# The sine product of k: from VectorE on PSUM to GpSimd on a copy in SBUF

## What is computed

```
q, k, v = split(x @ Wqkv)                 # 16 heads of 64
q = l2norm(q) * qs ;  k = l2norm(k) * ksc
q = q*cos*scale   + rotate_half(q)*sin*scale
k = k*cos/scale   + rotate_half(k)*sin/scale
out = softmax(8 * q k^T + mask) v         # window of 32, own and previous
x = out @ Wo + x ;  x = x + feed_forward(shift_tokens(x))
```

## Time and profile before

| | |
|---|---|
| median of 3 runs (lowest, highest) | 3969.29 us (3961.99, 3978.91) |
| the profiled execution | 3966.94 us |
| its span, first to last instruction | 3964.8 us |
| mean granted clock of TensorE, share of full speed | 0.975 |
| TensorE busy | 3450.3 us, 87% |
| VectorE busy | 3145.0 us, 79% |
| ScalarE busy | 2042.6 us, 52% |
| GpSimd busy | 2058.0 us, 52% |
| tiles, rounds of four tiles | 192, 48 |

### The profile page before, as it was taken

One profiled execution on the slowest core, in us unless ns is written; L12 is line 12 of the kernel. 1 busy time (PEld: TensorE's weight loads), 2 busy tenths in 40 slices (PEclk: granted clock), 3 DMA queues, 4 the chain that ended last, 5 costly groups with the idle time before them and its releaser, 6 DMA issues. The chain is left out here.

```text
span 3964.8 us, 101654 instructions
## 1 busy us (share of the span) xinstructions
PE 3450.3 (87%) x42643; PEld 2207.1 (56%) x42643; DVE 3145.0 (79%) x5766; ACT 2042.6 (52%) x3871; POOL 2058.0 (52%) x1073
## 2 busy tenths in 40 slices
PE   8998788888888889888889888888888888888886
PEld 4554455555555555555555555555555555555554
DVE  3334788888788888788888888888888888888885
ACT  2222355555555555555555555555555555555554
POOL 0000565656556555555556556555555565555562
PEclk9999899999999999999999999999999999999999
DMA  2000001000000000001000001000001000000000
GB/s 63 1 1 1 7 10 31 10 7 10 10 15 28 10 10 10 7 15 28 10 10 10 7 15 31 7 10 10 7 15 31 10 7 10 10 15 10 15 10 12
DMA packets 62282, 52.55 MB, mean 13 GB/s; under 512 B 11526, under 2 KB 59396, under 8 KB 61828
## 3 DMA queue, kind: packets, MB, share of 16 engines
q1 hardware_dynamic: 61828, 46.05, 4.3%
HBM read 43.93 MB, written 2.10 MB: 12 GB/s over the span
## 5 line engine op out<-in xcount | busy, mean ns | idle before, releaser
L412 POOL TENSOR_TENSOR cosp<-cosp,sinp 128x1024 f32<-128x1024 f32 x384 | 906.5, 2361 | 801.2 <-DVE sinp L826 801.2
L402 POOL TENSOR_TENSOR cosp<-cosp,rr 128x1024 f32<-128x1024 f32 x384 | 722.9, 1904 | 677.4 <-DVE rr L65 677.4
L694 ACT ACTIVATE sq<-ps 128x1024 f32<-128x1024 f32 x384 | 393.5, 1025 | 1231.1 <-DVE sinp L826 1231.1
L483 PE MATMUL ps<-w_qk,xs 128*128 128x512 f32 x1536 | 769.2, 624 | 51.2 <-ACT xs L683 46.9
L823 DVE TENSOR_TENSOR cosp<-ps,tab 128x1024 f32<-128x1024 f32 x384 | 469.1, 1222 | 386.3 <-PE ps L483 386.3
L588 PEld LDWEIGHTS ps<-px,w_vo 128*128 128x128 f32 x6144 | 715.2, 192 | 94.2 <-issue 89.6
L588 PE MATMUL ps<-px,w_vo 128*128 128x128 f32 x6144 | 717.5, 275 | 0.5
L490 PE MATMUL ps<-ident,cosp 128*128 128x128 f32 x3072 | 438.1, 300 | 308.1 <-DVE hh L846 168.6
L490 PEld LDWEIGHTS ps<-ident,cosp 128*128 128x128 f32 x3072 | 383.2, 155 | 348.5 <-issue 239.0
L483 PEld LDWEIGHTS ps<-w_qk,xs 128*128 128x128 f32 x1536 | 274.5, 199 | 406.0 <-issue 204.8
L826 DVE TENSOR_TENSOR sinp<-ps,tab 128x1024 f32<-128x1024 f32 x384 | 466.3, 1214 | 0.0
(11 more groups left out here) (102 smaller groups left out, 4038.3 us busy)
## 6 DMA issues: line engine op xcount, KB each, us to landing
tab<-in_tab SPq DMA_DIRECT2D x96, 128.0 KB, 2.0
qks<-in_scales SPq DMA_DIRECT2D x96, 128.0 KB, 3.4
w_qk<-in_L_ffn_Wqkv SPq DMA_DIRECT2D x12, 512.0 KB, 6.5
w_v<-in_wv_t SPq DMA_DIRECT2D x6, 512.0 KB, 8.2
w_o<-in_L_ffn_Wo SPq DMA_DIRECT2D x6, 512.0 KB, 9.3
x<-in_L_attn_x SPq DMA_DIRECT2D x16, 128.0 KB, 3.5
out<-w_v SPq DMA_DIRECT2D x16, 128.0 KB, 2.7
w<-in_L_ffn_W SPq DMA_DIRECT2D x6, 341.0 KB
```

Source lines behind the costliest of these rows:

```text
L402: eng.tensor_tensor(v, v, rr[:, B % 2, HEADS * i:HEADS * i + HEADS].unsqueeze(2).to_broadcast([P, HEADS, DH]), ALU.mult).then_inc(rot_read ...
L412: eng.tensor_tensor(cosp[:, A % 2, i, :], cosp[:, A % 2, i, :], sinp[:, i, :], ALU.add).then_inc(rot_added, 1)
L483: t = eng.matmul(ps[:, u, :], xs[:, n % ROUND, :], w_qk[:, n // TILES % 2, i, 512 * u:512 * u + 512], start=True, stop=True)
L694: eng.activation(sq[:, i, :], R.rearrange("p a n -> p (a n)"), ACT.Square).then_inc(sq_done, 1)
```

## The change

The sine product of k leaves VectorE's list. ScalarE copies k from `R` into a new SBUF tensor `kk` after the cosine product of k (`k_cos_done`, and the sine product of the tile before, `k_sin_done`), signals `k_evac`, and squares `kk` in place of `R`. GpSimd makes the sine product from `kk` between its two additions, waits for its own result and for the cosine product, and adds k. The next q projection waits for `k_evac` alone, and the table loads for both products of k.

```diff
@@ sync, load_table
-                    eng.wait_ge(k_roped, 2 * (ROUND * (T - 1) + 2 * w + 2))
+                    eng.wait_ge(k_cos_done, ROUND * (T - 1) + 2 * w + 2)
+                    eng.wait_ge(k_sin_done, ROUND * (T - 1) + 2 * w + 2)
@@ gpsimd, step
-                    for i, roped in enumerate((q_roped, k_roped)):
-                        eng.wait_ge(roped, 2 * A + 2)
-                        eng.tensor_tensor(cosp[:, A % 2, i, :], cosp[:, A % 2, i, :], sinp[:, i, :], ALU.add).then_inc(rot_added, 1)
+                    eng.wait_ge(q_roped, 2 * A + 2)
+                    eng.tensor_tensor(cosp[:, A % 2, 0, :], cosp[:, A % 2, 0, :], sinp[:, 0, :], ALU.add).then_inc(rot_added, 1)
+                    eng.wait_ge(k_evac, A + 1)
+                    after(eng, rot_added, 2 * A)
+                    sin = tab[:, A % ROUND // 2, 3, :].rearrange("p (u f) -> p u f", u=2).unsqueeze(1).to_broadcast([P, HEADS, 2, 32])
+                    eng.tensor_tensor(sinp[:, 1, :].rearrange("p (h u f) -> p h u f", u=2, f=32),
+                                      kk[:, :].rearrange("p (h u f) -> p h u f", u=2, f=32)[:, :, ::-1, :], sin, ALU.mult).then_inc(k_sin_done, 1)
+                    eng.wait_ge(k_cos_done, A + 1)
+                    eng.wait_ge(k_sin_done, A + 1)
+                    eng.tensor_tensor(cosp[:, A % 2, 1, :], cosp[:, A % 2, 1, :], sinp[:, 1, :], ALU.add).then_inc(rot_added, 1)
@@ tensor, step
-                    after(eng, k_roped, 2 * A)
-                    after(eng, sq_done, 2 * A)
+                    after(eng, k_evac, A)
@@ scalar
             def square(n, i):
-                eng.wait_ge((q_roped, k_roped)[i], 2 * n + 2)
                 after(eng, ssq_done, 2 * n - 1 + i)
-                eng.activation(sq[:, i, :], R.rearrange("p a n -> p (a n)"), ACT.Square).then_inc(sq_done, 1)
+                if i == 0:
+                    eng.wait_ge(q_roped, 2 * n + 2)
+                    eng.activation(sq[:, 0, :], R.rearrange("p a n -> p (a n)"), ACT.Square).then_inc(sq_done, 1)
+                else:
+                    eng.wait_ge(k_evac, n + 1)
+                    eng.activation(sq[:, 1, :], kk[:, :], ACT.Square).then_inc(sq_done, 1)
+
+            def take_k(n):
+                eng.wait_ge(k_cos_done, n + 1)
+                after(eng, k_sin_done, n)
+                eng.copy(kk[:, :], R.rearrange("p a n -> p (a n)")).then_inc(k_evac, 1)
...
                 if tile(A):
+                    take_k(A)
                     square(A, 1)
@@ vector, rope
-                eng.tensor_tensor(cosp[:, n % 2, i, :].rearrange("p (h d) -> p h d", d=DH), src, cos, ALU.mult).then_inc(roped, 1)
-                after(eng, rot_added, 2 * n - 1 + i)
-                swapped = R.rearrange("p a (h u f) -> p (a h) u f", u=2, f=32)[:, :, ::-1, :]
-                eng.tensor_tensor(sinp[:, i, :].rearrange("p (h u f) -> p h u f", u=2, f=32), swapped, sin, ALU.mult).then_inc(roped, 1)
+                eng.tensor_tensor(cosp[:, n % 2, i, :].rearrange("p (h d) -> p h d", d=DH), src, cos,
+                                  ALU.mult).then_inc((q_roped, k_cos_done)[i], 1)
+                if i == 0:
+                    sin = tab[:, w, 1, :].rearrange("p (u f) -> p u f", u=2).unsqueeze(1).to_broadcast([P, HEADS, 2, 32])
+                    after(eng, rot_added, 2 * n - 1)
+                    swapped = R.rearrange("p a (h u f) -> p (a h) u f", u=2, f=32)[:, :, ::-1, :]
+                    eng.tensor_tensor(sinp[:, 0, :].rearrange("p (h u f) -> p h u f", u=2, f=32), swapped, sin, ALU.mult).then_inc(q_roped, 1)
```

More of the change, by code:

```diff
@@ L132, in build @@
         sq = sb("sq", [P, 2, INNER])
+        kk = sb("kk", [P, INNER])
         ss = sb("ss", [P, 2 * HEADS + TB])
@@ L215, in build @@
         q_roped = sem("q_roped")
-        k_roped = sem("k_roped")
+        k_cos_done = sem("k_cos_done")
+        k_evac = sem("k_evac")
+        k_sin_done = sem("k_sin_done")
         sq_done = sem("sq_done")
@@ L815, in rope @@
             def rope(n, i):
-                roped = (q_roped, k_roped)[i]
                 w = n % ROUND // 2
@@ L819, in rope @@
                 cos = tab[:, w, 2 * i, :].unsqueeze(1).to_broadcast([P, HEADS, DH])
-                sin = tab[:, w, 2 * i + 1, :].rearrange("p (u f) -> p u f", u=2).unsqueeze(1).to_broadcast([P, HEADS, 2, 32])
                 eng.wait_ge((q_done, k_done)[i], n + 1)
                 after(eng, turned, 4 * (n - 2) + 2 + 2 * i)
-                eng.tensor_tensor(cosp[:, n % 2, i, :].rearrange("p (h d) -> p h d", d=DH), src, cos, ALU.mult).then_inc(roped, 1)
-                after(eng, rot_added, 2 * n - 1 + i)
-                swapped = R.rearrange("p a (h u f) -> p (a h) u f", u=2, f=32)[:, :, ::-1, :]
-                eng.tensor_tensor(sinp[:, i, :].rearrange("p (h u f) -> p h u f", u=2, f=32), swapped, sin, ALU.mult).then_inc(roped, 1)
+                eng.tensor_tensor(cosp[:, n % 2, i, :].rearrange("p (h d) -> p h d", d=DH), src, cos,
[5 more added lines that the diff above has]
+                    eng.tensor_tensor(sinp[:, 0, :].rearrange("p (h u f) -> p h u f", u=2, f=32), swapped, sin, ALU.mult).then_inc(q_roped, 1)
             def square_sum(n, i):
```

## The result

The changed kernel takes 4399.49 us (median of 4 runs, 4398.71 to 4400.33) beside 3965.64 us of the kernel before (4 runs, 3958.53 to 3978.91): 1.109 times as long, 95% interval 1.106 to 1.112. The loss is 434 us; the forecast was 289. The direction and the mechanism came as predicted, the size did not: the time stands at the upper end of the range. The profiled execution took 4400.33 us at a mean granted clock of 0.92, which was 0.975 before.

What follows compares the result with a forecast made beforehand. A loop through VectorE's k products and inverse roots and TensorE's transposes was taken to bound three of four steps; 3967 + 201 (roots waiting for GpSimd) + 88 (clock falls) = 4256 us, range 4100 to 4400.

Steps and rivals of the forecast that it cites:

- rivals 1 and 2: VectorE's root instructions run undisturbed beside GpSimd, 3908 us (chance 0.08); TensorE late by itself, so no change, 3967 us (0.03).
- rival 3: On GpSimd, the swapped order makes the sine product 3.4 us, so every delay grows by 1.04: 4444 us (chance 0.08).
- The forecast's holds: VectorE's inverse-root instructions wait for running GpSimd instructions to end: 4.19 us per round of four tiles, 201 us.
- the 1.07 that b was to hide: Root delay ahead of tiles with number modulo four 1, 1.07 us, hidden because TensorE comes late there from its own work.
- the clock term: Longer TensorE gaps lower the granted clock in every third and fourth step of a round, 1.67 us a fall: 88 us.
- the gap of a: TensorE's idle time before transposes in tiles with number modulo four 0, to grow from 1.54 to 3.1 us.

Runs made afterwards that it cites:

- the two runs at full clock: The changed kernel and the kernel before, each with matmuls without use in TensorE's gaps ahead of the transposes: 4179.10 us and 3905.37 us.
- the extra add: The kernel before with one more 128x1024 GpSimd addition, on data of its own, behind the add of k: 4271.36 us, ratio 1.073.

## Why the prediction was right in kind and short in size

**What came as worked out.** VectorE's gain was the 0.41 us of the wait for the scores and not the 1.22 of the instruction (0.44: the row maximum starts at 1.84 instead of 2.28). The sine product took 2.365 us (2.36 taken), copy and square 1.01 and 1.06 (1.03), and they cost nothing. L858 took 1.77 us and ended 7.25 us after the cosine product (7.16), L55 0.65 us in b and d. In c and d the transposes wait for the same releasers. So rivals 1 and 2 fall with line 858, rival 3 with line 419: its time, 4444, was nearly reached, but not by its mechanism.

**Where the 145 us went that were missing.** The stretches of rounds 2 to 46, averaged by step, grew from 73.13 to 82.21 us per round: 9.08 us, times 48 rounds 436, the loss within 2 us. The holds in this table come from the two runs at full clock (75.84 and 70.94), and the clock is what is left, with the few steps in which a layer changes or results leave. The forecast's holds are placed here in the step in which the root instructions run, less the 1.07 that b was to hide:

| step | holds, forecast | holds, measured | clock, forecast | clock, measured |
|---|---|---|---|---|
| a | 1.07 | 1.17 | 0 | 1.13 |
| b | 0.49 | 0.95 | 0 | -0.09 |
| c | 1.07 | 1.23 | 1.24 | 2.45 |
| d | 1.56 | 1.55 | 0.60 | 0.69 |
| sum per round | 4.19 | 4.90 | 1.84 | 4.18 |
| times 48 | 201 | 235 | 88 | 201 |

**The step that failed is the clock term**, 113 of the 147 us (436 less 289). Two things in it were mis-sized, about equally. A fall in c was priced at 1.67 us, from steps whose mean clock was 0.92. In the changed kernel a c with a fall takes 23.07 us against 20.10 without, 2.97: the clock averages 0.85, and both the transposes (3.65 us, 2.96 in the earlier trace rows) and the k projection behind them (3.20 us, 1.88 in d of the same round) run slow. The price of one fall was taken as fixed, but it is not; here it came with a gap of 4.28 us instead of 2.60. The gap alone doesn't set it: with the extra add, behind 4.12 us, the c shown above took 21.40 us at 0.92, with a k projection of 1.88 us.

And a was given no falls in the forecast, only 80 us at the upper end; it had them in 34 of 45 rounds, at 18.88 against 17.21 us. The forecast had put the gap of a at 3.1 us, more than the 2.60 of c, and by its own reason, that a longer gap went ahead of the falls, a belonged in the sum. The gap itself was misread: it was to grow ahead of the k transposes, as in the earlier trace rows (3.39 us), and instead a second one opened ahead of the q transposes, by a way over GpSimd's L406 that the forecast didn't follow. The clock fell behind these two gaps of 1.42 and 1.54 us too.

**The smaller miss is b.** It was to hide 1.07 us whole, because TensorE is late there from its own work. It hid about 0.7. The transposes of k in b, shown above, wait 0.27 us for VectorE's `xa` (L904), a second way from VectorE into that step which the forecast didn't look for. That is 0.46 us per round, 22 us; the rest of the misses in the holds, 0.10 in a and 0.16 in c, is in large part that GpSimd's add starts at 4.86 (median) and not 4.78, and in c not resolved further.

**That the time still lies in the range is in part luck.** The upper end counted 80 us of falls in a, of which 54 came, and 63 us for a slower sine product, of which nothing came. What took their place are the dearer falls in c (58 us) and the longer holds (34 us).

**What stays open:** why the clock falls in one step and not in another with nearly the same gap (d: 9 of 45 rounds at 3.39 us, 44 of 45 at 3.48), why a c with a fall takes 21.4 us in one kernel and 23.1 in another (gaps of 4.12 and 4.28 us), and why a change in d alone moved the falls to c. The falls can be counted, priced and prevented by these runs; neither they nor their price can be forecast from one gap's length.

## What to carry to other kernels

Before work is moved from VectorE to GpSimd, look at what VectorE does in the time into which GpSimd's queue will reach: a chain of tiny SBUF instructions there pays the rest of each GpSimd instruction that it meets, ten times its own duration in this case, and the record counts that wait as busy time, so the busy shares don't show it. Take the gain of a removed instruction from what its successor waits for next (0.41 us here, not 1.22). Where the bound engine idles in gaps, price the clock at each gap that grows, in every step and with the longer low stretch, or fill the gaps with idle matmuls first and count without it.

## What the runs showed of the hardware

- A GpSimd memset, which reads nothing, holds a TENSOR_SCALAR of 32 columns until 0.04 us after its own end (0.67 us instead of 0.18).
- Between two GpSimd instructions that follow at once, one held VectorE instruction slips in, and the next is held by the second one: L858 at 1.77 us, then L55 at 0.65.
- Ten and eight matmuls of 0.23 us in two idle gaps of a round gain 1.8% by the clock alone; and with some gaps shortened and others left, falls of the clock turn up in steps that nobody touched (c: 13 of 45 rounds, then 40).
